# A graph kernel's first attention sum: who weighs which head, and in what sets the last rows go

## What is computed

```python
for hd in range(H):                       # H = 4
    h = inputs * W[hd]
    logits = (h @ a[hd, :D])[src] + (h @ a[hd, D:])[dst]
    e = jnp.exp(jax.nn.leaky_relu(logits, 0.2))
    rowsum = jax.ops.segment_sum(e, src, num_segments=N)
    agg = jax.ops.segment_sum(e[:, None] * h[dst], src, num_segments=N)
    outs.append(jax.nn.elu(agg / rowsum[:, None]))
return jnp.mean(jnp.stack(outs, axis=-1), axis=-1)
```

## Time and profile before

| | us |
|---|---|
| median of 3 runs (lowest, highest) | 5078.98 (5077.45, 5080.45) |
| the profiled execution | 5069.63, its span 5067.9 |
| `sum_neighbours`: first gather to last add | 1201.3 to 1878.1 of the span |
| VectorE's adds (L1681): 416, busy | 290.9 |
| GpSimd's gathers (L1607): 416, busy | 456.9 |
| ScalarE's activations (L1698): 672 + 576, busy | 198.7 + 169.4 |
| VectorE's head-0 steps (L1664): 28 + 24, busy | 34.7 + 29.6 |

### The profile page before, as it was taken

The page is one execution under the profiler, slowest core; times in us unless marked ns, Lnnn a source line. Parts: engine busy times, 40 slices in busy tenths (PEclk is TensorE's granted clock), DMA queues, the critical chain, the costliest instruction groups (busy, mean ns, idle before and its releaser), DMA issues. The chain is left out here.

```text
span 5067.9 us, 46827 instructions
## 1 busy us (share of the span) xinstructions
PE 1669.7 (33%) x10711; PEld 944.4 (19%) x10711; DVE 2841.0 (56%) x4778; ACT 1640.9 (32%) x4317; POOL 2024.4 (40%) x1847
## 2 busy tenths in 40 slices
PE   3133200100000000001543433522222237899989
PEld 2022200100000000000111111111111127644444
DVE  5728667781677779871333333564777775722131
ACT  1312301110656657001544333513444454310010
POOL 0055777706777710027123444126767642000000
PEclk9566555555555555555666665665555568999999
DMA  3000000005666620002011122226778736578856
GB/s 120 19 12 1 3 1 1 1 0 163 169 181 186 185 49 0 0 20 51 17 38 44 54 59 56 51 72 199 246 233 251 239 78 178 193 278 271 269 169 211
DMA packets 215383, 553.41 MB, mean 109 GB/s; under 512 B 46177, under 2 KB 112411, under 8 KB 214404
## 3 DMA queue, kind: packets, MB, share of 16 engines
q0 software_dynamic: 99984, 272.83, 19.9%
q1 hardware_dynamic: 115188, 278.18, 16.1%
HBM read 485.70 MB, written 65.20 MB: 109 GB/s over the span
## 5 line engine op out<-in xcount | busy, mean ns | idle before, releaser
L1171 POOL DMA_INDIRECT blend_got<-rec,blend_slot x416 | 394.8, 949 | 539.7 <-DVEq L1214 407.4
L900 POOL DMA_INDIRECT table<-edges_record,edges_place x391 | 512.8, 1311 | 142.9 <-issue 123.6
L2691 PE MATMUL fourth_bank<-fourth_tile,fourth_z 128*128 128x512 f16 (+1 forms) x2800 | 559.8, 361 | 19.8 <-DVEq L2852 10.1
L2053 POOL DMA_INDIRECT heads_got<-rec,heads_slot x416 | 466.8, 1122 | 183.8 <-issue 124.4
L244 PE MATMUL blend_count<-blend_mov,blend_stat 128*128 x980 | 351.2, 440 | 562.0 <-issue 461.6
L1607 POOL DMA_INDIRECT sum_got<-rec,sum_slot x416 | 456.9, 1098 | 157.3 <-issue 124.9
L1223 DVE TENSOR_SCALAR blend_mov<-built_iota_low,built_low 128x800 f16 x490 | 213.0, 435 | 516.2 <-issue 318.0
L1681 DVE TENSOR_TENSOR rounds_y<-rounds_y,sum_got 128x516 f32 x416 | 290.9, 699 | 124.7 <-issue 34.8
L1251 ACT ACTIVATE blend_gap<-built_iota_ten,built_offset 128x128 f32 x490 | 196.8, 402 | 493.4 <-issue 392.4
L200 PE MATMUL edges_p_key<-kept_ident,edges_key_row 128*128 128x128 f32 x4 | 1.1, 428 | 1035.6 <-DVEq L167 1035.6
L2691 PEld LDWEIGHTS fourth_bank<-fourth_tile,fourth_z 128*128 128x128 f16 x2800 | 261.7, 99 | 311.6 <-issue 15.0
(11 more groups left out here) (666 smaller groups left out, 4394.7 us busy)
## 6 DMA issues: line engine op xcount, KB each, us to landing
fourth_tile<-cs SPq DMA_DIRECT2D x100, 800.0 KB, 4.4
fourth_tile<-ct SPq DMA_DIRECT2D x100, 800.0 KB, 4.3
ct<-blend_cst SPq DMA_DIRECT2D x20, 1000.0 KB
heads_counts<-ct SPq DMA_DIRECT2D x25, 800.0 KB
cs<-heads_flipped SPq DMA_DIRECT2D x25, 800.0 KB
attend_cnt<-ct SPq DMA_DIRECT2D x50, 256.0 KB
sort_low_wide<-low SPq DMA_DIRECT2D x4, 3136.0 KB
attend_cnt<-ct SPq DMA_DIRECT2D x25, 288.0 KB
```

What stands on the lines that cost most here:

```text
L900: pool.indirect_dma_start(table, bass.IndirectOffsetOnAxis(ap=K["place"][0:lanes, t:t + 1], axis=0), K["record"][0:lanes, t, :], None).the ...
L1171: pool.indirect_dma_start(got[:, buf, r, :], None, rec_dram, bass.IndirectOffsetOnAxis(ap=slot[:, t:t + 1], axis=0)).then_inc(gathered[buf ...
L2053: pool.indirect_dma_start(got[:, buf, r, :], None, rec_dram, bass.IndirectOffsetOnAxis(ap=slot[:, t:t + 1], axis=0)).then_inc(gathered[buf ...
L2691: last = pe.matmul(bank[m][:, 0:w], z2[s % 2][:, k, part, :], tile[:, n % RING, at:at + w], start=(k == 0 and part == 0), stop=(k == NB - ...
```

## The change

In sets of 32 rows ScalarE weighs all four heads of a row, four activations instead of three, and VectorE has no head-0 step. The exponentials of the next set still start behind row 12, but in three steps a row (42 steps at most shared out over the rows that are left). The sets are now twelve of 32 rows, then one of 16 and two of 8. In the last three (SHARED) head 0 is weighed by VectorE, as before, and ScalarE has three heads. Within them the steps of the next set start behind the first row: three a row in the set of 16, six a row in the first set of 8. A set of 16 has two parts and so 35 steps, a set of 8 has 34, on as many fewer rows. The parts, the ring, the gathers and their waits stay as they are.

```diff
--- before.py
+++ after.py
@@ -1549,14 +1549,15 @@
 
 
 
-    SETS, ROWS = 13, SLOT_ROWS // 13
-    PARTS = 4
-    PART = ROWS // PARTS
-    HELD = 8
-    ON_ACT = 3
+    PART, HELD = 8, 8
+    ROWS = 32
+    SETS = [ROWS] * 12 + [16, 8, 8]
+    FIRST = [sum(SETS[:n]) for n in range(len(SETS))]
+    SHARED = 3
     FIRST_EXP = 12
+    EXP_STEPS = 42
     heads, F1 = y.shape[2], y.shape[3]
-    rest = heads - ON_ACT
+    last_sets = len(SETS) - SHARED
     live, slot = c.sb("live", [P, SLOT_ROWS]), c.sb("slot", [P, SLOT_ROWS], I32)
     ends = live[0:PARTS3, :]
     chunk_row = c.sb("chunk_row", [1, SLOT_ROWS], I32)
@@ -1596,7 +1597,7 @@
         def _(pool):
             pool.iota(when_i[:, :], [[1, SLOT_ROWS]], base=0, channel_multiplier=0).then_inc(counting, 1)
             pool.wait_ge(ready, 1)
-            for part in range(PARTS * SETS):
+            for part in range(SLOT_ROWS // PART):
                 if part == HELD - 1:
 
                     pool.wait_ge(turned, 3)
@@ -1644,34 +1645,38 @@
 
             def weigh(n):
 
-                l, *tmp = small
-                at = slice(n * ROWS, (n + 1) * ROWS)
-                for part in range(PARTS * n, PARTS * (n + 1)):
+                rows, first = SETS[n], FIRST[n]
+                l, *tmp = (tile[:, :, 0:rows] for tile in small)
+                for part in range(first // PART, (first + rows) // PART):
                     wait_gathered(dve, part)
-                    logits = l[:, :, part % PARTS * PART:(part % PARTS + 1) * PART]
+                    logits = l[:, :, part * PART - first:(part + 1) * PART - first]
                     step(dve.tensor_tensor(logits, own[:, :, part * PART:(part + 1) * PART],
                                            got[:, rows_of(part), heads * F1:RECORD].rearrange("p r k -> p k r"), ALU.add))
                     yield
                 step(dve.scalar_tensor_tensor(l, l, 0.2, l, ALU.mult, ALU.max))
                 yield
-                yield from exp_once(step, dve, l, live[:, at].unsqueeze(1).to_broadcast([P, heads, ROWS]), weights[n % 2], tmp)
+                yield from exp_once(step, dve, l, live[:, first:first + rows].unsqueeze(1).to_broadcast([P, heads, rows]),
+                                    weights[n % 2][:, :, 0:rows], tmp)
                 dve.sem_inc(factors, 1)
 
-            def weigh_first_head(part):
-
-                rows = got[:, rows_of(part), 0:rest * F1]
-                e = weights[part // PARTS % 2][:, 0, part % PARTS * PART:(part % PARTS + 1) * PART]
-                step(dve.tensor_tensor(rows, rows, e.unsqueeze(2).to_broadcast([P, PART, rest * F1]), ALU.mult))
+            def weigh_first_head(n, r):
+
+                rows = got[:, rows_of((FIRST[n] + r) // PART), 0:F1]
+                e = weights[n % 2][:, 0, r:r + PART]
+                step(dve.tensor_tensor(rows, rows, e.unsqueeze(2).to_broadcast([P, PART, F1]), ALU.mult))
 
             for _ in weigh(0):
                 pass
-            for n in range(SETS):
-                exps = weigh(n + 1) if n + 1 < SETS else iter(())
-                for r in range(ROWS):
-                    t = n * ROWS + r
+            for n, rows in enumerate(SETS):
+                exps = weigh(n + 1) if n + 1 < len(SETS) else iter(())
+                from_row = FIRST_EXP if rows == ROWS else 0
+                per_row = -(-EXP_STEPS // (rows - from_row))
+                for r in range(rows):
+                    t = FIRST[n] + r
                     if r % PART == 0:
                         dve.reg_load(regs, chunk_row[0:1, t:t + PART])
-                        weigh_first_head(PARTS * n + r // PART)
+                        if n >= last_sets:
+                            weigh_first_head(n, r)
                     at_chunk = dve.snap(regs[r % PART], min_val=0, max_val=NB - 1)
                     sums = y[:, bass.ds(at_chunk, 1), :, :].rearrange("p a k f -> p (a k f)")
 
@@ -1679,22 +1684,23 @@
                     if t >= 1:
                         dve.wait_ge(added, t)
                     dve.tensor_tensor(sums, sums, got[:, t % (HELD * PART), 0:heads * F1], ALU.add).then_inc(added, 1)
-                    if r >= FIRST_EXP:
-                        next(exps, None)
-                        next(exps, None)
+                    if r >= from_row:
+                        for _ in range(per_row):
+                            next(exps, None)
                 for _ in exps:
                     pass
 
         @block.scalar
         def _(act):
-            for n in range(SETS):
+            for n, rows in enumerate(SETS):
                 half = n % 2
                 act.wait_ge(factors, n + 1)
-                for r in range(ROWS):
+                for r in range(rows):
+                    t = FIRST[n] + r
                     if r % PART == 0:
-                        wait_gathered(act, PARTS * n + r // PART)
-                    for k in range(rest, heads):
-                        part = got[:, (n * ROWS + r) % (HELD * PART), k * F1:(k + 1) * F1]
+                        wait_gathered(act, t // PART)
+                    for k in range(1 if n >= last_sets else 0, heads):
+                        part = got[:, t % (HELD * PART), k * F1:(k + 1) * F1]
                         last = act.activation(part, part, ACT.Copy, scale=weights[half][:, k, r:r + 1])
                     last.then_inc(weighed, 1)
```

## The result

The changed kernel takes 5128.66 us (median of 5 runs, 5109.51 to 5136.44), the kernel before beside it 5080.45 (5077.45 to 5085.06): a ratio of 1.0102 with a 95% interval of 1.0085 to 1.0119. The forecast was 5057, in a range of 5028 to 5088. The profiled execution of after took 5128.66 (span 5126.9), 59 us more than that of before.

What follows compares the result with a forecast made beforehand. VectorE was taken to set the pace by its own order of work; 1767.8 + 38.3 + 50.1 = 1856.2 ends the sum, 22 us sooner than 1878.3, giving a median of 5057 us, range 5028 to 5088.

Steps and rivals of the forecast that it cites:

- Step (1): VectorE's own work in a 32-row set: without head-0 weighing it falls by 5.4 us to 41.2 us.
- nine rows of 1.84: VectorE's rows with three exponential steps after row 13: 1.84 us each, part of an 18.8 us sum.
- step (4): Ring of gathers tying GpSimd to VectorE: two parts plus landing make a set 44.0 us, VectorE waiting 2.8.
- Step (2): ScalarE with the fourth head: 128 activations, 37.6 us a set; it stays ahead of VectorE at no cost.
- the cold start: ScalarE's first set: seven activations 1.40 us apart, 1.00 idle before 0.40 of work; eats that set's gain.
- Rival (d): ScalarE's instructions come 1.40 us apart, so the factors' lead is gone: same or slower; slower outcomes together 0.15.
- Rival (a): VectorE alone bounds the sets at 41.2 us each: 50 us less, 5028.6 us; chance 0.14.
- Rival (c): Gathers lock to the three-step rows in parts 1 and 2: 51.6 us a set, 5136; slower outcomes together 0.15.
- Step (3): Three exponential steps a row from row 12 end in row 24 instead of 30, giving ScalarE its lead.
- step 4: VectorE's fourth logits step, at row 13 of a set, which needs the next set's fourth gathered part landed.
- Step (5): End of the sum: twelfth set 38.3 us, then sets of 16, 8 and 8 rows 50.1, 16 us more than now.

Runs made afterwards that it cites:

- the run with three heads: Changed kernel with ScalarE weighing only heads 1 to 3 in the full sets too, head 0 weighed by nobody: 5120.11 us, 1.0097 of the kernel before.
- the 13-set version: Changed kernel with 13 sets of 32 rows, head 0 on VectorE in the last set alone: 0.9922 of the kernel before (4333.48 us), on another chip 1.0084.

## Why the prediction was wrong, step by step

Forecast end of the sum 1856.2, measured 1938.6: 82 us. The start of the twelfth set was forecast at 1767.8 and came at 1847.7 (80 of the 82); that set took 42.2 instead of 38.3 (4 more), the last 32 rows 48.7 instead of 50.1 (1 less). Two steps failed, the row's pace and ScalarE's lead, and the run with three heads shows that the first is enough by itself for nearly all of the loss (sets of 50.5 us instead of 51.7).

- **Step (1), VectorE's own set, failed in its three-step rows**, and with it the "nine rows of 1.84" of step (4). Where dispatch is quick they hold: twelve plain rows in 11.0 us, three-step rows at 1.84, rows 24 to 31 in 7.7. But with ScalarE 7 to 10 rows ahead, in the run with three heads, rows 12 to 23 still take 28 to 34 us instead of some 22, because VectorE's own control instructions take 0.70 us there. The sum has no term for them.
- **Step (2) failed**: "It stays ahead; cost nothing." Where nothing slows the dispatch it is nearly so: 128 activations in 37.6 us, and 2.1 us of waiting a set. In the changed kernel they come at 0.7 and 1.4 us for some 20 us a set, and of VectorE's idle time about as much ends with ScalarE's signal (42 us) as comes with its own slow instructions (48). I had read the cold start as belonging to the first set.
- **Rival (d) named this very interval, 1.40 us**, and I dismissed it by "96 in a row at 0.294 in every later set". Those rows came from a kernel in which the step to be removed held up the gathers four times a set. The run without only that step shows that the evidence went with it. I gave (d) no price, and it spoke of ScalarE alone; slow dispatch on both engines was worth 77 us over sets 1 to 10 (517 us instead of 440).
- **Rival (a)** is summed from 1327.5, where ScalarE's set 1 starts; the first add of that set comes at 1330.4, so its sum is 3 us short. Nothing hangs on it.
- **Rival (c)** came out near the measured time (5136) by luck, for a wrong reason: in the three-step rows the gathers are 0.94 or 0.95 us long with 0.30 between, and don't lock to the row.
- **Step (3)** is harmless by itself: with head 0 back on VectorE, three steps and small sets included, the ratio is 1.0027.
- **Step (4), the ring's loop**, is right where it could be seen: 43.5 us a set on the quick chip, with VectorE waiting 1.24 us a set for the landing at step 4 (forecast 2.8); in sets 1 to 10 of the changed kernel it waits for the landing only 3 times, 3.1 us in all.
- **Step (5)**: 48.7 for 50.1. That 13 sets of 32 would be better by some 10 us is not shown: 1.0084 and 1.0076 on a chip with slow stretches can't be told apart. On the quick chip the changed kernel was not run. Worked out from the 13-set version there (47.3 and 32.9 for its last two sets) and from 40.2 and 48.7 for those rows of the changed kernel elsewhere, it would take 8.7 us more, some 4342 us or 0.994, which is the sign and about the size of the forecast. That is argued, not shown.

What is shown: on the chips that have slow stretches, they go with GpSimd gathering some 20 us or more without a stop or a long hold (10 us or more where activations have one column); pauses take them away, VectorE's two-input operations on SBUF take them away (1.24 us, four a set) or shorten them (0.60 us, eight a set), and the same time on PSUM does not. What stays open is how GpSimd's gathering slows the dispatch of other engines, and why on one chip it doesn't. Nor does any run tell whether the recording of instructions by the profiler has a part in it. The fetch of instructions would be one candidate: but its packets are as many on the quick chip as on the slow (132, 1.08 MB), and the trace of after dates them. From 1446.1 to 1469.1, the slow stretch of set 3, the list of DMA queues has one line (packets, MB, share of the 16 engines):

```profile
q0 software_dynamic: 1353, 4.49, 69.1%
```

These are the gathers'. No packet of an instruction queue starts in these 23 us, nor in the slow stretch of set 4 (1499.3 to 1524.1), so it isn't fetches under way that hold the engines up. The Trainium skill (Runtime: NRT & Kernel Launch, "Instruction fetch mechanics") has each sequencer fetch its code through a DMA queue of its own ahead of need, so that fetching is hidden by issue. The trace agrees in so far as the slow instructions of those two stretches had no fetch beside them; by that rule, too, the stretches would not be slow for want of code. That issue alone costs up to 1.0 us between two activations is what the rows show.

## What to carry to other kernels

Before one engine's idle time is put down to another, run it with the other far ahead: here VectorE stayed nearly as slow with ScalarE 7 rows in front. Before an operation is taken off one engine, ask what it did to the others while it ran: here 1.24 us of VectorE, four times a set, held up GpSimd's gathers, and where dispatch could turn slow that was worth about what it cost. A steady rate read from a trace (0.294 us an activation) holds for the company in which it was read; where the same trace shows the same instruction at 1.40 us elsewhere, price that rate as a rival. And run a change of under 1% on more than one chip: the 13-set version is 0.9922 of before on one and 1.0084 on another.

## What the runs showed of the hardware

- One program took 4333 us on one chip and 5084 on another, with nearly equal busy times; gaps between instructions marked "issue" make up much of the difference, on TensorE, VectorE and ScalarE. Three other chips showed them, the one of 4333 us did not.
- Where such gaps come, the starts of short instructions lie 0.70 or 1.40 us apart (0.40 us of work, 0.30 or 1.00 idle), whatever their size: with one column of 129 as well (0.29 of work, 0.42 or 1.11 idle). Instructions of control on VectorE take 0.70 us instead of 0.02 to 0.06.
- The slow stretch of set 3 passed without one packet on an instruction queue.
- Gathers can run undisturbed beside VectorE's adds at 0.95 us with 0.30 between; half the bytes or half the rows don't change the slow stretches.
